# Two sums over 100,000 edges of a graph network: float32r parts, groups of four chunks, setup between steps, five parts

## The chip, the cores and the metric

The kernel runs on one core of one Trainium2 chip. The metric is the device time of one execution in microseconds (us). Three runs of the kernel before gave 4151.52, 4155.08 and 4159.06 us; the median is 4155.08.

## The reference

Four graph layers on 3125 nodes with 32 features share 100,000 edges (`src`, `dst`). Each layer takes `h = relu(layernorm(x))` and adds its result to `x`:

```
L0:  agg[src[e]] += edge_attr_32[e]                       # 32 values per edge
     x += batchnorm(relu([h, agg] @ W1.T + b1)) @ W2.T + b2
L1:  R = relu(edge_weight * w1 + b1) @ w2 + b2            # per edge, 64 -> 320
     msg = R combined with spherical harmonics of edge_attr_3 and h[src[e]]
     x[dst[e]] += msg                                     # 32 values per edge
L2:  3 rounds: out = clip(0.9 * segment_sum(norm * out[src], dst) + 0.1 * h, 0, 1)
L3:  3 rounds: z = batchnorm(relu(segment_sum(wn * z[src], dst)))
```

`norm` holds weights and weighted degrees, `wn` holds plain degrees.

## The kernel before, in words

The edges are padded to 784 chunks of 128 (an edge is a partition, a chunk is a column), and four chunks are a step: 196 steps in each of two loops. NP is 3200, the padded count of nodes.

**First sum** (`phase0` of each engine). A node number is split into a high part `a` (13 values) and a low part `b` (256 values). ScalarE makes a one-hot row of `b` for each edge in `onehots` (L510): four Squares of the distance to `iota_b`, then one Relu over the four. VectorE makes, in `products` (L921, L925), the edge's 32 values placed at its `a`: 13 x 32 = 416 columns. TensorE multiplies the two in `scatter` (L674, L678), one product for each of two parts of 128 nodes, and accumulates in PSUM. All buffers have two slots, and step s waits for the use of step s - 2.

**Matrix entries.** Beside this, the edges are written into a dense matrix `both` in HBM (two numbers for each pair of nodes: a count and a weight). GpSimd adds them by indirect DMAs with addition, one DMA per chunk (L433). Two edges of one DMA, or of DMAs in flight together, must not add to the same entry. So equal pairs of nodes inside a pair of chunks are merged first: `compare` on ScalarE (L496) makes the matrix of equal keys from a row of keys that SP loads broadcast over the partitions (L329), `mark_earlier` on VectorE (L896) finds the first of each, `merge` on TensorE (L658) sums the weights, `entries` and `entry_places` on VectorE (L905, L916) write values and places. One pair of chunks is merged per step, in both loops together 392. `add_pair` on GpSimd (L427) waits for its places and until the pair before has been added. GpSimd starts when ScalarE's queue has zeroed `both` in 40 pieces (L473): four first, then one per step. It adds 150 pairs (FIRST), then waits for the feature table.

**Between the loops** come the dense part of L0 (L942 to L998), the layer norm, and the store of a table of node features to HBM (L340).

**Second sum** (`phase1`). GpSimd gathers the features of each edge's source, one indirect DMA per chunk (L443, four per step), and between them adds pairs: two pairs per step until it has caught up with the merging, then one. TensorE forms `R` in `radial` (L715, L721), VectorE multiplies it with the features (L1020, L1024) and reduces (L1034), and `products` and `scatter` sum the messages by `dst`, now with four parts of 128 low values and 7 high values, 7 x 34 = 238 columns.

After it, `both` is read, split and used in six rounds of dense products for L2 and L3 (L749, L799).

VectorE's setup before the first loop (L855 to L894) makes keys, `a` and `b` of both ends, the three bf16 parts of the weights, `stack_id`, the layer norm of x and the unit directions `rdir`. `s_edge` fires after all of it, and ScalarE and TensorE wait for it.

## Time and profile before

| | |
|---|---|
| profiled execution | 4156.54 us, span 4154.5 us |
| granted TensorE clock, mean | 0.936 of 2.4 GHz |
| TensorE busy (PE) | 3650.0 us, 88% |
| VectorE busy (DVE) | 2566.9 us, 62% |
| ScalarE busy (ACT) | 2213.9 us, 53% |
| GpSimd busy (POOL) | 2133.7 us, 51% |
| HBM read, written | 360.07 MB, 151.93 MB |

Times in rows are us from the start of the span unless marked ns. Matmuls are pipelined, and a busy TensorE is not one at its peak. An fp32 matmul of the code appears as two recorded matmuls. GpSimd's row of an indirect DMA is the time in which it writes the descriptors, and the transfer follows it. Idle time stands behind a row in brackets, with what ended it.

### The profile page before, as it was taken

What the parts mean: (1) busy time and instruction counts of PE and PEld (TensorE: products, weight loads), DVE (VectorE), ACT (ScalarE), POOL (GpSimd) and SP (SyncE); (2) the same over time, 40 slices, a digit from 0 to 9 for tenths busy, and PEclk for the clock granted to TensorE, in tenths of its full rate; (3) what the DMA queues carried; (4) which work ended last, traced back from release to release, by engine and by line L of the source; (5) the groups of instructions that cost most, each with busy time, mean ns of one, the idle gap of its engine ahead of it and who ended that gap; (6) DMA issues with size and microseconds to landing.
All of it is one profiled execution on the core that took longest, in us unless ns stands there. A gap on an engine that the chain in (4) does not pass through costs nothing.

```text
span 4154.5 us, 65664 instructions
## 1 busy us (share of the span) xinstructions
PE 3650.0 (88%) x15883; PEld 2396.3 (58%) x15883; DVE 2566.9 (62%) x6324; ACT 2213.9 (53%) x3662; POOL 2133.7 (51%) x1582
## 2 busy tenths in 40 slices
PE   5999999999978888889999999999999754576776
PEld 2555555555546666668888888888888411132222
DVE  6555555555547776679999999999999511101011
ACT  4776776666735555557767676767666311300000
POOL 0025555555508888888888888888888300000000
PEclk9999999999988888889999999999999988778877
DMA  8962222222212222222222222222222599978764
GB/s 296 387 237 35 34 34 34 34 35 34 35 33 39 35 34 35 35 39 49 49 49 49 49 49 49 49 49 49 49 49 49 212 426 425 412 287 343 305 252 193
DMA packets 293088, 512.62 MB, mean 123 GB/s; under 512 B 153191, under 2 KB 228584, under 8 KB 275128
## 3 DMA queue, kind: packets, MB, share of 16 engines
q1 hardware_dynamic: 132232, 323.63, 21.8%
q0 software_dynamic: 137984, 39.44, 12.1%
q10 hardware_dynamic: 22832, 149.10, 8.6%
q8 instruction: 14, 0.23, 0.0%
q14 instruction: 26, 0.21, 0.0%
HBM read 360.07 MB, written 151.93 MB: 123 GB/s over the span
## 4 chain that ended last, share of the span: by engine, by line
PE 36%; DVE 24%; issue 14%; DMA 13%; POOL 9%; DVEq 2%; ACTq 1%; ACT 1%; SPq 0%; POOLq 0%
PE ps L678 28%; DVE kept L1024 7%; PE ps L749 6%; POOL both L433 6%; DVE kept L1034 4%; DMA adj_c<-kept 4%; POOL kept L443 3%; DMA big<-adj_c 3%; DVE prod L925 3%; DMA both<-kept 2%; DVE kept L1020 2%; DMA big<-both 1%; PE ps L785 1%; DMA adj_c<-prod 1%; DMA big<-adj_w 1%
## 5 line engine op out<-in xcount | busy, mean ns | idle before, releaser
L678 PE MATMUL ps<-prod,big 128*128 128x238 f32 (+1 forms) x9408 | 2518.6, 426 | 92.7 <-DVE prod L925 80.4
L678 PEld LDWEIGHTS ps<-prod,big 128*128 128x128 f32 x9408 | 1804.6, 195 | 717.5 <-issue 517.9
L433 POOL DMA_INDIRECT both<-kept x784 | 1289.9, 1645 | 805.3 <-DMA both<-kept 297.5
L520 ACT ACTIVATE big<-big 128x1024 f32<-128x1024 f32 (+1 forms) x392 | 581.5, 1483 | 877.2 <-PE ps L678 825.2
L443 POOL DMA_INDIRECT kept<-feat_dram,kept x784 | 839.1, 1070 | 331.2 <-issue 167.8
L515 ACT ACTIVATE big<-iota_b,kept 128x256 f32<-128x256 f32 (+1 forms) x1568 | 830.4, 600 | 0.0
L721 PE MATMUL ps<-w2mix,kept 65*128 65x384 f32 x1568 | 564.1, 502 | 29.9 <-ACT kept L555 20.7
L1034 DVE TENSOR_REDUCE kept<-kept 128x80 f32<-128x1280 f32 x392 | 561.5, 1472 | 0.0
L925 DVE SCALAR_TENSOR_TENSOR prod<-iota_a,kept,attr 128x416 f32<-128x416 f32 x784 | 475.5, 647 | 46.3 <-DMA attr<-in_ea 27.8
L1024 DVE TENSOR_TENSOR kept<-ps,kept 128x384 f32<-128x384 f32 x784 | 395.6, 545 | 0.0
L721 PEld LDWEIGHTS ps<-w2mix,kept 65*128 65x128 f32 x1568 | 283.3, 191 | 193.3 <-issue 33.3
L502 ACT ACTIVATE kept<-kept 128x256 f32<-128x256 f32 x784 | 350.0, 493 | 67.5 <-DMA kept<-keys_dram 56.0
L911 DVE TENSOR_REDUCE kept<-ps 128x12 f32 (+1 forms) x392 | 64.0, 163 | 509.4 <-PE ps L669 498.0
L749 PE MATMUL ps<-big,zring 128*32 128x512 f32 (+1 forms) x1120 | 243.8, 604 | 114.6 <-DMA big<-adj_c 49.0
L925 DVE SCALAR_TENSOR_TENSOR prod<-iota_a,kept 128x238 f32<-128x238 f32 x784 | 313.1, 462 | 46.9 <-DVE kept L1043 28.5
L799 PE MATMUL ps<-big,zring 128*32 128x512 f32 (+3 forms) x400 | 187.9, 624 | 164.0 <-DMA big<-both 149.9
L1020 DVE TENSOR_TENSOR kept<-ps,kept 128x512 f32<-128x512 f32 x392 | 266.4, 680 | 0.0
L1078 DVE COPY prod<-ps 128x512 f32<-128x512 f32 x18 | 11.3, 684 | 409.7 <-PE ps L749 403.7
L507 ACT ACTIVATE kept<-kept 128x512 bf16<-128x512 f32 x392 | 247.0, 630 | 28.5
L749 PEld LDWEIGHTS ps<-big,zring 128*32 128x32 f32 x1120 | 74.1, 119 | 278.6 <-issue 250.1
L799 PEld LDWEIGHTS ps<-big,zring 128*32 128x32 f32 x400 | 45.7, 125 | 306.3 <-issue 286.9
L593 ACT ACTIVATE kept<-big 128x1600 f32<-128x1600 f32 x50 | 82.4, 1653 | 248.4 <-issue 142.9
(147 smaller groups left out, 1606.8 us busy)
## 6 DMA issues: line engine op xcount, KB each, us to landing
both<-big ACTq DMA_DIRECT2D x40, 2000.0 KB, 9.1
big<-both SPq DMA_DIRECT2D x50, 1600.0 KB, 12.6
big<-adj_c SPq DMA_DIRECT2D x48, 1600.0 KB, 9.9
big<-adj_w SPq DMA_DIRECT2D x32, 1600.0 KB, 10.1
kept<-keys_dram SPq DMA_DIRECT2D x392, 128.0 KB
adj_c<-kept ACTq DMA_DIRECT2D x42, 800.0 KB, 37.6
adj_w<-kept ACTq DMA_DIRECT2D x32, 800.0 KB, 36.7
kept<-in_wT SPq DMA_DIRECT2D x196, 128.0 KB
```

The costliest lines, as they stand in the source:

```text
L433: pool.indirect_dma_start(both, bass.IndirectOffsetOnAxis(ap=sc_idx[:, 2 * d + j:2 * d + j + 1], axis=0), sc_val[:, d, j, :], None, bounds ...
L443: pool.indirect_dma_start(gath[:, s % 2, k, :], None, feat_dram, bass.IndirectOffsetOnAxis(ap=src_i[:, 4 * s + k:4 * s + k + 1], axis=0), ...
L502: act.activation(key_gap[:, i, :], keyrow[:, q, :], ACT.Square, scale=-1.0, bias=key[:, ds(2 * d + i, 1)]).then_inc(s_gap, 1)
L515: act.activation(dist2[:, k, 0:wide], iota_b[:, 0:wide], ACT.Square, scale=-1.0, bias=bcol[:, ds(4 * s + k, 1)]).then_inc(s_dist[n], 1)
L520: act.activation(onehot[:, q, :, 0:wide], dist2[:, :, 0:wide], ACT.Relu, scale=-1.0, bias=1.0).then_inc(s_oh[n], 1)
L678: mm = pe.matmul(part_sums(n, part, width), onehot[:, q, k, part * P:(part + 1) * P], prod[:, q, k, 0:HI[n] * width], start=False, stop=Fa ...
L721: mm = pe.matmul(ps[:, 4 + k, 0:384], hidT[:, q, k * P:(k + 1) * P], w2mix[:, :], start=True, stop=True)
L749: mm = pe.matmul(ps[g:g + 32, n, 0:w], zring[:, m % 8, :], values[:, c0:c0 + w], start=(m < 4), stop=(m >= NA - 4), skip_group_check=True)
L925: V.scalar_tensor_tensor(out=prod[:, q, k, 0:HI[n] * width].rearrange("p (a m) -> p a m", a=HI[n]), in0=iota_a[:, 0:HI[n]].unsqueeze(2).br ...
L1020: V.tensor_tensor(T[:, :, 0:256].rearrange("p k (o x) -> p k o x", o=16), ps[:, 4 + 2 * g:6 + 2 * g, 0:256].rearrange("p k (o x) -> p k o ...
L1024: ins = V.tensor_tensor(T[:, k, 256:640].rearrange("p (u i x) -> p u i x", u=8, i=3), ps[:, 4 + 2 * g + k, 256:384].rearrange("p (u x) -> ...
L1034: V.tensor_reduce(res[:, q, 2 * g:2 * g + 2, 0:40], terms[:, g, :, :].rearrange("p k (o x) -> p k o x", x=16), AX, ALU.add).then_inc(s_red, 1)
```

## The change

1. `PARTS` goes from (2, 4) to (2, 5): the second sum has 5 parts of 128 low values (640) and 5 high values, 5 x 34 = 170 columns.
2. In the first sum each float32 value is split by VectorE into a high part (the lower 12 bits cleared) and the rest; both are placed (13 x 64 = 832 columns), and TensorE multiplies each with the one-hot as float32r. `prod0` and `onehot0` are float32r tensors that lie over memory the first loop doesn't use otherwise.
3. In the first loop, groups of four chunks are merged in every second step. ScalarE compares half a group per step, two chunks against 512 keys. The second loop keeps pairs. GpSimd adds four chunks without waiting between them, 88 groups before the table. The spare rows go from 2 x 128 to 4 x 128.
4. `s_edge` fires after the weight parts. Destination parts and `stack_id` follow step 0, the layer norm step 1, the squares of the directions step 2, the reciprocal and `rdir` step 3. SP loads x and the directions after two attribute loads, the weights after four. ScalarE starts the zeroing when the index and weight loads have landed, no more when the keys are in HBM. Two memsets move behind the first loop.

```diff
-PARTS = (2, 4)
+PARTS = (2, 5)
-FIRST = 150
+FIRST = 88
+            def load_group(g, slot):
+                if not first(g):
+                    sp.wait_ge(s_gap, 4 * (g - 1))
+                row = keys_dram[ds(4 * g, 4), :].rearrange("(o c) p -> o (c p)", o=1)
+                sp.dma_start(keyrow[:, slot, :], row.broadcast_to([P, 4 * P])).then_inc(s_krow[slot], 16)
-            def add_pair(d):
-                pool.wait_ge(s_idx, d + 1)
-                if d:
-                    pool.wait_ge(s_add, 32 * d)
-                for j in range(2):
-                    ...
+            def add(first_c, n):
+                pool.wait_ge(s_idx, (first_c + n) // 2)
+                if first_c:
+                    pool.wait_ge(s_add, 16 * first_c)
+                for c in range(first_c, first_c + n):
+                    pool.indirect_dma_start(both, bass.IndirectOffsetOnAxis(ap=sc_idx[:, c:c + 1], axis=0),
+                                            sc_val[:, c // 2, c % 2, :], None, bounds_check=last_entry,
+                                            compute_op=ALU.add).then_inc(s_add, 16)
-            for d in range(FIRST):
-                add_pair(d)
+            for g in range(FIRST):
+                add(4 * g, 4)
             for s in range(STEPS):
+                if s + 1 < STEPS:
+                    gather(s + 1, (0, 1))
+                n = 4 if added < CH // 2 else 2
+                if added + n <= 2 * (STEPS + s + 1 - BEHIND):
+                    add(added, n)
+                    added += n
+                if s + 1 < STEPS:
+                    gather(s + 1, (2, 3))
+                if CH // 2 <= added <= 2 * (STEPS + s - BEHIND):
+                    add(added, 2)
+                    added += 2
+            def compare_group(g, s, slot, half):
+                ...
+                for i in (2 * half, 2 * half + 1):
+                    act.activation(key_gap[:, i % 2, :], keyrow[:, slot, :], ACT.Square, scale=-1.0,
+                                   bias=key[:, ds(4 * g + i, 1)]).then_inc(s_gap, 1)
+                act.wait_ge(s_gap, 2 * s + 2)
+                if half == 0 and not first(g):
+                    act.wait_ge(s_ded, 2 * g - 2)
+                act.activation(same[:, slot, 2 * half:2 * half + 2, :], key_gap[:, :, :], ACT.Relu, scale=-1.0,
+                               bias=1.0).then_inc(s_same, 1)
+            def merge_group(g, slot):
+                ...
+                for j in range(4):
+                    pe.matmul(o[:, j, 0:1], same_tri[:, slot, j, :], ones_bf[:, :], ...)
+                    for i in range(4):
+                        mm = pe.matmul(o[:, j, lo:7], same[:, slot, i, j * P:(j + 1) * P], ...)
             def scatter(n, s, q, k, width):
                 ...
+                    else:
+                        for t in range(2):
+                            mm = pe.matmul(part_sums(n, part, width), onehot0[:, q, k, mine],
+                                           prod0[:, 4 * q + k, :, t, :], start=False, stop=False,
+                                           skip_group_check=True)
+            def split_products(s, q, k):
+                if not first(s):
+                    dve.wait_ge(s_sum[0], 4 * s - 8 + k + 1)
+                V.scalar_tensor_tensor(
+                    out=prod0[:, 4 * q + k, :, :, :].rearrange("p a t m -> p a (t m)"),
+                    in0=iota_a[:, 0:HI[0]].unsqueeze(2).broadcast_to([P, HI[0], 2 * FEAT]),
+                    scalar=a_src[:, ds(4 * s + k, 1)],
+                    in1=rows0[:, q, k, :, :].rearrange("p t m -> p (t m)").unsqueeze(1)
+                    .broadcast_to([P, HI[0], 2 * FEAT]),
+                    op0=ALU.is_equal, op1=ALU.mult).then_inc(s_prod[0], 1)
+            def phase0(s, k4, u):
+                q, g, slot = k4 % 2, u * 2 + k4 // 2, k4 // 2
+                if q:
+                    mark_group(g, slot)
+                dve.wait_ge(s_attr[q], 32 * u + 16 * slot + 16)
+                V.tensor_scalar(rows0[:, q, :, 0, :].bitcast(I32), attr[:, q, :, :].bitcast(I32), -4096, None,
+                                ALU.bitwise_and).then_inc(s_hi, 1)
+                dve.wait_ge(s_hi, s + 1)
+                V.tensor_tensor(rows0[:, q, :, 1, :], attr[:, q, :, :], rows0[:, q, :, 0, :],
+                                ALU.subtract).then_inc(s_rows, 1)
+                dve.wait_ge(s_rows, s + 1)
+                for k in range(4):
+                    split_products(s, q, k)
+                    if q and k == 2:
+                        group_entries(g, slot)
+                if q:
+                    group_places(g)
```

`mark_group`, `group_entries` and `group_places` are `mark_earlier`, `entries` and `entry_places` over four chunks.

## Rows read from the trace of the kernel before

**Rows 1.** Timeline, one step of the first sum: start us, us, engine, line.

```profile
601.69 5.83 PE L678 MATMUL ps<-prod,big 128*128 128x416 f32 x16
602.99 0.28 DVE L902 TENSOR_TENSOR kept<-kept,earlier 128x256 bf16<-128x256 bf16 x1
603.19 1.77 DVE L925 SCALAR_TENSOR_TENSOR prod<-iota_a,kept,attr 128x416 f32<-128x416 f32 x3
603.77 0.63 ACT L507 ACTIVATE kept<-kept 128x512 bf16<-128x512 f32 x1
604.31 1.69 ACT L515 ACTIVATE big<-iota_b,kept 128x256 f32<-128x256 f32 x4
607.51 5.83 PE L678 MATMUL ps<-prod,big 128*128 128x416 f32 x16
```

**Rows 2.** Windows: stretch, length, busy PE, PEld, DVE, ACT, POOL, PEclk, DMA share, GB/s.

```profile
60.00:260.00 200.00, 200.00 (x761) 109.49 (x759) 103.50 (x277) 141.72 (x272) 0.00 (x0) 1.00 0.96 381
1213.00:1224.00 11.00, 10.37 (x49) 10.37 (x49) 1.45 (x8) 0.00 (x0) 0.00 (x0) 0.50 0.01 1
2000.00:3000.00 1000.00, 1000.00 (x4880) 812.65 (x4880) 967.03 (x2441) 698.86 (x1062) 806.00 (x637) 1.00 0.29 49
```

**Rows 3.** Timeline of GpSimd where the second sum turns to single pairs.

```profile
1824.19 1.09 POOL L443 DMA_INDIRECT kept<-feat_dram,kept  x1 [0.31 <-issue]
...
1829.61 1.62 POOL L433 DMA_INDIRECT both<-kept  x1 [0.30 <-issue]
...
1833.42 1.10 POOL L443 DMA_INDIRECT kept<-feat_dram,kept  x1 [0.31 <-issue]
```

**Rows 4.** Timeline of GpSimd: first and last add ahead of the table, first gather.

```profile
268.84 1.69 POOL L433 DMA_INDIRECT both<-kept  x1 [263.27 <-DMA both<-big]
...
1146.55 1.66 POOL L433 DMA_INDIRECT both<-kept  x1 [0.30 <-issue]
1240.38 1.10 POOL L443 DMA_INDIRECT kept<-feat_dram,kept  x1 [92.17 <-DMA feat_dram<-big]
```

**Rows 5.** Timeline: the dense part's first operation, the last gather.

```profile
1195.88 0.99 DVE L945 COPY big<-h 128x800 f32<-128x800 f32 x1 [4.90 <-PE ps L678]
...
3249.24 1.05 POOL L443 DMA_INDIRECT kept<-feat_dram,kept  x1 [0.30 <-issue]
```

**Rows 6.** Timeline of TensorE: bf16 opening, small fp32 products, second sum.

```profile
1208.84 0.61 PE L654 MATMUL ps<-zero_bf 128*128 128x512 bf16 x2
1213.63 10.88 PE L711 MATMUL ps<-w2T,big 128*128 128x32 f32 x50 [4.18 <-DVE big L967]
...
2206.58 6.69 PE L678 MATMUL ps<-prod,big 128*128 128x238 f32 x32
```

**Rows 7.** Groups by line and shape, whole span: count, busy us, mean ns.

```profile
L515 ACT ACTIVATE big<-iota_b,kept 128x512 f32<-128x512 f32 x784 | 499.3, 707 | 0.0
L925 DVE SCALAR_TENSOR_TENSOR prod<-iota_a,kept,attr 128x416 f32<-128x416 f32 x784 | 475.5, 647 | 46.3 <-DMA attr<-in_ea 27.8 <-PE ps L678 3.1
L515 ACT ACTIVATE big<-iota_b,kept 128x256 f32<-128x256 f32 x784 | 331.0, 493 | 0.0
L925 DVE SCALAR_TENSOR_TENSOR prod<-iota_a,kept 128x238 f32<-128x238 f32 x784 | 313.1, 462 | 46.9 <-DVE kept L1043 28.5 <-issue 18.2
```

**Rows 8.** Timeline of the setup: the last weight part, the last directions.

```profile
21.88 1.68 DVE L877 CAST kept<-big 128x784 bf16<-128x784 f32 x1
...
44.26 2.61 DVE L892 TENSOR_TENSOR kept<-big 128x2352 f32<-128x2352 f32 x1
```

**Rows 9.** DMA issues from 60 to 260 us: count, KB each, median us to landing.

```profile
both<-big ACTq DMA_DIRECT2D x34, 2000.0 KB, 9.0
```

**Rows 10.** Timeline of GpSimd and VectorE around two adds of the first loop.

```profile
560.12 1.54 POOL L433 DMA_INDIRECT both<-kept  x1 [0.30 <-issue]
...
562.60 1.78 DVE L925 SCALAR_TENSOR_TENSOR prod<-iota_a,kept,attr 128x416 f32<-128x416 f32 x3
...
563.94 1.84 POOL L433 DMA_INDIRECT both<-kept  x1 [2.28 <-DMA both<-kept]
```

More of the change, by code:

```diff
@@ L19 @@
 F32 = mybir.dt.float32
+F32R = mybir.dt.float32r
 BF16 = mybir.dt.bfloat16
@@ L179, in gnn_program, with placed_at @@
         big = sb("big", [P, 4, NP])
+        big_end = nc.sbuf_base
+        def placed_at(name, shape, end):
+            n = 4
+            for d in shape[1:]:
+                n *= d
+            return nc.alloc_sbuf_tensor_at(name, shape, F32R, offset=end - n)
+        prod0 = placed_at("prod0", [P, 8, HI[0], 2, FEAT], kept_end)
+        onehot0 = placed_at("onehot0", [P, 2, 4, PARTS[0] * P], big_end - 4 * (2 * NP - 2 * 4 * PARTS[0] * P))
         zeros = big[:, 0, :]
@@ L336, in load0 @@
                              ea32_in[:, ds(s * (4 * FEAT), 4 * FEAT)]).then_inc(s_attr[q], 16)
-            steps(sp, load0)
+            for s in range(2):
+                load0(s, s, 0)
+            sp.dma_start(x[:, :, :], x_in.rearrange("(a b) f -> b a f", b=P)).then_inc(s_in["x"], 16)
+            sp.dma_start(rel[:, :, :], ea3_in).then_inc(s_in["rel"], 16)
+            for s in range(2, 4):
+                load0(s, s, 0)
+            for dst, src in loads:
+                sp.dma_start(dst, src).then_inc(s_in["wts"], 16)
+            with sp.Fori(1, STEPS // 4) as u:
+                for k4 in range(4):
+                    load0(u * 4 + k4, k4, u)
             sp.wait_ge(s_table, 1)
@@ L560, in phase1 @@
                 onehots(1, s, q, b_dst)
+            act.wait_ge(s_edge, 2)
             steps(act, phase1)
@@ L660, in merge @@
                 pe.wait_ge(s_tri, d + 1)
-                if not first(d):
-                    pe.wait_ge(s_idx, d - 1)
+                pe.wait_ge(s_idx, d - 1)
                 o = ps[:, 2 + q, 0:14].rearrange("p (j v) -> p j v", j=2)
@@ L894, in _, with mark_group @@
-            dve.wait_ge(s_edge, 1)
+            V.tensor_copy(wparts[:, :, 6], wrest).then_inc(s_edge, 1)
+            dve.wait_ge(s_edge, 1)
+            def mark_group(g, slot):
+                dve.wait_ge(s_same, 2 * g + 2)
+                if not first(g):
+                    dve.wait_ge(s_ded, 2 * g - 2)
+                within = same[:, slot, :, :].rearrange("p i (j e) -> p (i j) e", j=4)[:, 0:16:5, :]
+                V.tensor_tensor(same_tri[:, slot, :, :], within,
+                                earlier[:, :].unsqueeze(1).broadcast_to([P, 4, P]), ALU.mult).then_inc(s_tri, 2)
@@ new lines, in group_entries @@
+            def group_entries(g, slot):
+                dve.wait_ge(s_ded, 2 * g + 2)
+                if not first(g, 1):
+                    dve.wait_ge(s_idx, 2 * g)
+                m = ps[:, 2 + slot, 0:28].rearrange("p (j v) -> p j v", j=4)
+                V.tensor_reduce(sc_val[:, ds(2 * g, 2), :, :].rearrange("p d j v -> p (d j) v"),
+                                m[:, :, 1:7].rearrange("p j (v i) -> p j v i", i=3), AX, ALU.add)
+                V.scalar_tensor_tensor(out=offs[:, :], in0=m[:, :, 0], scalar=0.0, in1=to_spare[:, ds(4 * g, 4)],
+                                       op0=ALU.is_gt, op1=ALU.mult).then_inc(s_offs, 2)
@@ new lines, in _ @@
+            dve.wait_ge(s_keysd, 16)
+            phase0(0, 0, 0)
+            link(V.tensor_scalar(tmp_i, dst_i[:, :], 7, None, ALU.arith_shift_right))
+            link(V.tensor_scalar(b_dst.bitcast(I32), tmp_i, 205, None, ALU.mult))
+            link(V.tensor_scalar(tmp_i, b_dst.bitcast(I32), 10, None, ALU.arith_shift_right))
+            link(V.tensor_copy(a_dst[:, :], tmp_i))
+            V.scalar_tensor_tensor(out=b_dst[:, :], in0=a_dst[:, :], scalar=-640.0, in1=dst_i[:, :],
+                                   op0=ALU.mult, op1=ALU.add).then_inc(s_edge, 1)
@@ new lines, in _ @@
+            link(V.tensor_tensor(stack_id[:, :], ident[:, 0:32], ident[:, 32:64], ALU.add))
+            link(V.tensor_tensor(stack_id[:, :], stack_id[:, :], ident[:, 64:96], ALU.add))
+            link(V.tensor_tensor(stack_id[:, :], stack_id[:, :], ident[:, 96:128], ALU.add))
+            phase0(1, 1, 0)
+            dve.wait_ge(s_in["x"], 16)
+            layernorm()
+            phase0(2, 2, 0)
+            dve.wait_ge(s_in["rel"], 16)
+            link(V.tensor_tensor(rinv[:, :], rel[:, :, 0], rel[:, :, 0], ALU.mult))
@@ L943, in _ @@
+            link(V.tensor_tensor(rdir[:, :, 2:5], rel[:, :, :],
+                                 rinv[:, :].unsqueeze(2).broadcast_to([P, CH, 3]), ALU.mult))
+            with dve.Fori(1, STEPS // 4) as u:
+                for k4 in range(4):
+                    phase0(u * 4 + k4, k4, u)
             dve.wait_ge(s_in["wts"], 16 * 12)
             dve.wait_ge(s_sum[0], CH)
+            V.memset(res[:, :, :, 41:42], 1.0)
+            link(V.memset(hidT[HID1:HID1 + 1, :, :], 1.0))
             V.tensor_copy(cat[:, :, 0:32], h[:, :, :])
```

217 lines of the change are left out of this document (109 added, 108 removed).

## The prediction

> **What bounds the kernel now.** I read the busy tenths of the page first, then the windows, the waits of each engine, the timelines of single steps, and last GpSimd's queue from end to end. The page's totals name TensorE (3650.0 of 4154.5 us), and the chain's largest line is its product L678 (28%); both mislead, for the loops have different limits.
>
> *First sum (196 steps, L686).* The next step's 16 passes begin 5.82 us after this one's [rows 1], and TensorE is busy in all 200 us of 60 to 260 [rows 2]. One fp32 product of 416 columns is two recorded passes, 5.83/16 = 0.35 us each, two clocks a column. VectorE and ScalarE have slack, GpSimd adds pairs beside them.
>
> *Second sum (196 steps, L729).* Here VectorE is busy 967 and GpSimd 806 of 1000 us [rows 2], and GpSimd's indirect DMAs follow each other with a gap of only 0.30 us, so its queue is full although the share says 81%. Its own pace for a step of four gathers and two adds is 1833.42 - 1824.19 = 9.23 us; the two adds take 1833.42 - 1829.61 = 3.81 of it, so an add costs 1.905 and a gather (9.23 - 3.81)/4 = 1.355 us [rows 3]. 106 steps in the 1000 us make 9.43 a step. Before that, 43 steps carry four adds each (L457 lets GpSimd catch up), and VectorE idles for gathers.
>
> So one queue runs through both loops. GpSimd waits for zeroed memory until 268.84, does 150 pairs until 1148.2, waits for the feature table until 1240.38 [rows 4], and its last gather ends at 3250.3 [rows 5]. Between: 784 gathers (1062 us) and 478 adds (911) are 1973 us of 2010; 37 are holds and waits. What comes later (904 us) the change leaves alone.
>
> **The first sum's step after.** *TensorE* has 16 float32r passes of 416 columns. No row shows this type. Lower bound: two bf16 products of 512 columns take 0.61 us in all [rows 6], near one clock a column, which would be 416/2.4 = 0.17 us here; upper bound: a pass as now, 0.35. I take 0.18, nearer to bf16, because float32r is given only numbers already cut to a short part, and a single product of it is to do what two passes did. That is 2.9 us, with ten small products a step (six cost 5.82 - 16 x 0.35 = 0.2 now) 3.2; at the upper bound 6.0. The Trainium skill ("FP8 and Floating Point Precision", TensorE Precision Notes) says that true fp32 takes four passes and reduced precision truncates to 22 bits; that counts two clocks a column in each of the two rows recorded, and by it the step is 3.2.
>
> *VectorE.* Products start 0.566 us apart at 416 elements ((1.77 - 0.65)/2 [rows 1]), and an element costs 1.04 ns ((647 - 462)/178 [rows 7]). Of 832 elements: 1.00 us, four 4.0. Two linked operations of 128 elements form the parts: nearest row 0.28 each [rows 1], with the link 0.6 (bounds 0.3 and 0.8). Marking and entries, once in two steps but on four chunks, about 0.42 a step. Sum 5.03 us.
>
> *ScalarE.* Compare now squares 512 columns: they start 0.614 apart (256 columns: (1.69 - 0.49)/3 = 0.40 [rows 1]; a column (707 - 493)/256 = 0.84 ns [rows 7]), so both with 0.07 of link make 1.39; the Relu over 1024 columns then keeps the engine 0.96 (512 columns: 0.54 [rows 1]); four squares of 256 take 1.72, their Relu 0.96. Sum 5.03 too. With two slots per buffer neither blocks the other much; I take 5.08 a step, bounds 4.9 (an engine runs ahead) and 5.5 (they wait in turn).
>
> *Setup.* `s_edge` fires after the weight parts: VectorE ends them at 23.56 now, less four casts of 0.6, at 21.2; it was at 46.9 [rows 8]. But stack_id, layer norm, squares, reciprocal and directions move between steps 0 to 3, still on VectorE, which is the bound now: 46.9 - 23.6 plus the destination columns, 25.5 us. Its cover is gone, so nothing is gained but the early start of TensorE. Step 4 begins near 21.2 + 25.5 + 4 x 5.03 = 67, say 70 with first loads. On SP the loads of x and of directions now follow two attribute loads, the weights' follow four; they land long before their users.
>
> *Zeroing* puts one piece of 2 MB per step into steps 4 to 39; until 260 the DMA engines are busy 96% [rows 2] at 5.83 us a step, 5.6 us of work. Faster steps don't make these transfers faster: 5.7 a step, last piece issued near 70 + 35 x 5.7 = 270, zeroed at about 276 (bounds 257 and 285; a piece lands in 9.0 us [rows 9]).
>
> End of the sum: 70 + 36 x 5.7 + 156 x 5.08 = 1068. The dense part from 1195.88 to the first gather is 44.5 us; the moved memsets add 1 on VectorE. Table ready: 1113.
>
> **The adds (FIRST = 88 groups).** GpSimd waits for the adds in flight once per four instead of once per two. One add is 1.54 and 0.30 [rows 10], the wait 2.2 to 2.3: 3 x 1.84 + 1.54 + 2.2 = 9.26 us. A pair should be 5.6 so, but 150 took 879.4, 5.86 each. Rows 10 show why: the add at 560.12, with no product of VectorE under its start, took 1.54; that at 563.94 began inside the third product from 562.60 and took 1.84, that is, it was held until the product ended at 564.38. Holds are 0.13 us per add now. After, products are 1.08 instead of 0.65 us long and fill 80% of VectorE's time instead of 40%; a random start finds 0.3 to 0.4 left, the following adds start a little before a product's end, 0.15 to 0.25. I take 0.21 per add, a group at 10.1 us; bounds 9.45 (0.05 each) and 10.9 (0.4 each). 88 groups: 889 us, less 8 for the stretch after VectorE's products have ended. 276 + 881 = 1157, later than the table (1113): the adds bind. The Trainium skill ("SBUF — State Buffer", SBUF: two separate sides) has a port pair that VectorE with two SBUF inputs and a GpSimd operation reading SBUF take for a whole instruction; the trace agrees (0.30 us more), and it speaks against this change, since one longer product holds longer. Without it the group would be 9.26 and the table would bind.
>
> **The second sum.** TensorE: five products of 170 columns a chunk, two passes each, instead of four of 238. A pass of 238 is at most 6.69/32 = 0.21 us [rows 6], 0.203 by columns (238/1.2 ns + 5); of 170, 0.147. Each pass loads 128 columns of weights: with hardly any columns to stream that took 10.88/50 = 0.218 us [rows 6] at a granted clock of 0.50 (1.2 GHz) [rows 2], so by an estimate 0.109 at full clock, below 0.147. 40 x 0.147 against 32 x 0.203: 0.6 us less, about 8.7 a step. Were it 0.218 here, a step would be 11.5 us and the time 1157 + 2254 + 904 + 2 = 4317; the full clock of [rows 2] in this loop, where TensorE stays 94% busy, speaks against it. VectorE: 4 x 68 x 1.04 ns = 0.28 less, 9.15. ScalarE: 4 x 128 + 512 columns more, 0.85 us, with 301 of 1000 us free. All are below GpSimd's 9.23, so GpSimd sets this loop; the gain per single step is 9.43 - 9.3, not TensorE's 0.6. Its work is what counts: 352 adds done before, so 426 up to the last gather instead of 478, and 16 steps with more than two adds instead of 43. 1062 + 426 x 1.905 = 1874, holds 19 (37 now), 1893 us (bounds 1874 and 1920).
>
> **Sum.** Last gather 1157 + 1893 = 3050 against 3250.3; the last step is half a microsecond shorter. The profiled execution's 4156.5 (span 4154.5 and 2.0 around it; median 4155.1) becomes **3956**.
>
> **Rivals.** *Holds fade.* For: the second to fourth add of a group may all start as one product ends. Against: the hold in [rows 10], on a shorter product. Group 9.45, adds end at 1108, the table binds at 1113: last gather 3006, 3912 us. *TensorE stays the bound in the first sum*: float32r passes at 0.35, or the clock falls to 1.2 GHz because TensorE works 3.2 of 5.1 us, which gives 416/1.2 = 0.35 as well. For: the granted clock is full only where it is always busy; against: its pauses would be below 1 us. 6.0 us a step: about 70 + 192 x 6.0 = 1222, table 1267, last gather 3160, 4066 us. *GpSimd is starved* (the other side): each add waits out a whole 1.0 us product. Group 9.26 + 4.0 = 13.3, first gather 1443, last 3336, 4242 us. It turns slower when a group costs over (1357 - 276)/88 = 12.3 us, a hold of 0.76 per add; the rows show 0.3 at most of a 0.65 product, which is against it.
>
> **How the numbers follow.** Forecast 0.60, holds fade 0.16, TensorE bound 0.16, starved or bound by weight loads 0.04, the rest (the same mechanisms, other sizes) 0.04. The forecast alone spans 3910 (zeroed at 257, group 9.9) to 4010 (285, 10.6). Range 3885 to 4070, which takes in the first two rivals. About 0.2% can be told from no change; faster 0.94, same 0.01, slower 0.05.
>
> **What would show it.** Steps of the first sum 5.0 to 5.2 us apart after 280, VectorE and ScalarE above 95% there and TensorE's recorded products near 0.18 apart; first add at 270 to 285; groups of four 10.1 us apart with adds of 1.6 to 1.9; last add of the first loop near 1157 and the first gather right behind it with no wait for the table; 16 steps of 13 us, then steps of 9.25 to 9.35 with VectorE waiting for gathers. It is wrong if the first gather waits for the table, if float32r passes are 0.35, or if single steps keep 9.43.

## The result, and the profile after

The changed kernel took **3977.2 us** (median of four runs, 3961.4 to 3986.6) against 4155.6 us of the kernel before: a ratio of 0.9567 with a 95% interval of [0.9535, 0.9599]. The profiled execution took 3975.5 us (span 3973.8); the forecast was 3956, so it is 19.5 us late, and the median 21.2.

First the page of the changed kernel: engine totals and three of its costliest groups.

```profile
PE 3210.8 (81%) x18235; PEld 2332.3 (59%) x18235; DVE 2874.9 (72%) x6330; ACT 2549.9 (64%) x3663; POOL 2152.9 (54%) x1582
...
L461 POOL DMA_INDIRECT both<-kept x784 | 1300.4, 1659 | 701.6 <-DMA both<-big 263.5
...
L470 POOL DMA_INDIRECT kept<-feat_dram,kept x784 | 847.6, 1081 | 239.2 <-issue 180.1
...
L1016 DVE SCALAR_TENSOR_TENSOR prod<-iota_a,kept,prod 128x832 fp32r<-128x832 f32 x784 | 805.9, 1080 | 48.7 <-DVE prod L1032 47.8
```

TensorE has lost 439 us of its 3650, the profiled time only 181. The windows (columns as in [rows 2], which holds the ones of before) tell where the limits lie:

```profile
60.00:260.00 200.00, 149.90 (x896) 118.16 (x894) 174.21 (x278) 173.56 (x279) 0.00 (x0) 0.91 0.96 386
600.00:1000.00 400.00, 342.34 (x2061) 238.43 (x2059) 377.35 (x630) 389.63 (x632) 267.34 (x154) 1.00 0.32 39
2000.00:3000.00 1000.00, 951.66 (x5777) 797.73 (x5776) 952.35 (x2461) 798.27 (x1070) 804.34 (x642) 0.99 0.32 49
```

In the first sum ScalarE is busy 389.6 and VectorE 377.4 of 400 us (with the 20 us that it waits for its own parts, L1032, it is full too), TensorE 342.3: its bound has passed to the two others, at 5.08 us a step (by the starts of VectorE's products). In the second sum 642 GpSimd instructions stand in 1000 us, six a step: 9.35 us a step, against 9.43.

GpSimd's queue from end to end, to be laid beside [rows 4, 5] (timeline: start, us, and in brackets what it waited for):

```profile
269.18 2.49 POOL L461 DMA_INDIRECT both<-kept  x1 [263.49 <-DMA both<-big]
...
1178.91 1.54 POOL L461 DMA_INDIRECT both<-kept  x1 [0.30 <-issue]
1180.76 1.09 POOL L470 DMA_INDIRECT kept<-feat_dram,kept  x1 [0.31 <-issue]
```

The first gather follows the last add with no wait for the table, as forecast, and the last gather starts at 3072.7. Four stretches make up the account:

| stretch | forecast | measured |
|---|---|---|
| zeroed, first add | 276 | 269.2 |
| 352 adds up to the first gather | 881 | 911.6 |
| first to the end of the last gather | 1893 | 1893.0 |
| from there to the end of the span | 904 less 0.5 | 900.0 |

So the miss is one term: the adds, 30.6 us too dear, less 6.8 for the earlier zeroing and nearly 4 at the end.

### The profile page after: what moved, and what is told of

Read it like the earlier page. It is cut to its first block, busy times and chain, and to the rows that moved or that the text cites. A ratio compares the mean times of both kernels' runs of the same rounds, so it can differ in the third digit from the quotient of the medians.

```text
span 3973.8 us, 69047 instructions
## 1 busy us (share of the span) xinstructions
PE 3210.8 (81%) x18235; PEld 2332.3 (59%) x18235; DVE 2874.9 (72%) x6330; ACT 2549.9 (64%) x3663; POOL 2152.9 (54%) x1582
## 4 chain that ended last, share of the span: by engine, by line
POOL 38%; DMA 35%; issue 13%; PE 9%; DVE 3%; ACT 1%; ACTq 0%; another core or an unknown queue 0%; SPq 0%; DVEq 0%; POOLq 0%
POOL both L461 22%; DMA both<-kept 21%; POOL kept L470 16%; PE ps L827 7%; DMA adj_c<-kept 4%; DMA big<-adj_c 2%; DMA big<-both 2%; DVE prod L1016 1%; PE ps L863 1%; DMA attr<-in_ea 1%; DMA big<-adj_w 1%; DMA adj_c<-prod 1%; PE ps L750 1%; DMA kept<-keys_dram 1%; DMA adj_w<-kept 1%
## 5 line engine op out<-in xcount | busy, mean ns | idle before, releaser
L745 PE MATMUL ps<-prod,big 128*128 128x170 f32 x7840 | 1221.8, 317 | 119.9 <-DVE prod L1006 119.8
L745 PEld LDWEIGHTS ps<-prod,big 128*128 128x128 f32 x7840 | 1172.4, 195 | 238.9 <-DVE prod L1006 229.1
L750 PE MATMUL ps<-prod,onehot 128*128 128x416 f32 x3136 | 776.9, 385 | 222.7 <-ACT onehot L564 123.3
L559 ACT ACTIVATE big<-iota_b,kept 128x256 f32<-128x256 f32 (+1 forms) x1568 | 914.8, 654 | 0.0
L1016 DVE SCALAR_TENSOR_TENSOR prod<-iota_a,kept,prod 128x832 fp32r<-128x832 f32 x784 | 805.9, 1080 | 48.7 <-DVE prod L1032 47.8
L750 PEld LDWEIGHTS ps<-prod,onehot 128*128 128x128 f32 x3136 | 553.2, 194 | 420.0 <-DVE prod L1016 369.7
L564 ACT ACTIVATE big<-big 128x2560 f32<-128x2560 f32 x196 | 458.0, 2337 | 376.2 <-PE ps L745 376.2
L799 PE MATMUL ps<-w2mix,kept 65*128 65x384 f32 x1568 | 564.0, 503 | 24.3 <-ACT kept L604 20.5
L1006 DVE SCALAR_TENSOR_TENSOR prod<-iota_a,kept 128x170 f32<-128x170 f32 x784 | 258.1, 392 | 56.2 <-DVE kept L1177 56.1
L546 ACT ACTIVATE kept<-kept 128x512 f32<-128x512 f32 x392 | 259.2, 708 | 20.7 <-DMA kept<-keys_dram 20.1
## 6 DMA issues: line engine op xcount, KB each, us to landing
big<-both SPq DMA_DIRECT2D x50, 1600.0 KB, 12.3
big<-adj_w SPq DMA_DIRECT2D x32, 1600.0 KB, 10.1
```

The source lines that it names most:

```text
L559: act.activation(dist2[:, k, 0:wide], iota_b[:, 0:wide], ACT.Square, scale=-1.0, bias=bcol[:, ds(4 * s + k, 1)]).then_inc(s_dist[n], 1)
L564: act.activation((onehot0, onehot)[n][:, q, :, 0:wide], dist2[:, :, 0:wide], ACT.Relu, scale=-1.0, bias=1.0).then_inc(s_oh[n], 1)
L745: mm = pe.matmul(part_sums(n, part, width), onehot[:, q, k, mine], prod[:, q, k, 0:HI[n] * width], start=False, stop=False, skip_group_che ...
L750: mm = pe.matmul(part_sums(n, part, width), onehot0[:, q, k, mine], prod0[:, 4 * q + k, :, t, :], start=False, stop=False, skip_group_chec ...
L799: mm = pe.matmul(ps[:, 4 + k, 0:384], hidT[:, q, k * P:(k + 1) * P], w2mix[:, :], start=True, stop=True)
L1016: V.scalar_tensor_tensor(out=prod0[:, 4 * q + k, :, :, :].rearrange("p a t m -> p a (t m)"), in0=iota_a[:, 0:HI[0]].unsqueeze(2).broadcast ...
```

## Why a group of adds takes two steps

This is the timeline of one group, VectorE and GpSimd together, in order of time:

```profile
514.39 1.08 DVE L1016 SCALAR_TENSOR_TENSOR prod<-iota_a,kept,prod 128x832 fp32r<-128x832 f32 x1
514.72 2.19 POOL L461 DMA_INDIRECT both<-kept  x1 [2.26 <-DMA both<-kept]
516.27 4.07 DVE L1016 SCALAR_TENSOR_TENSOR prod<-iota_a,kept,prod 128x832 fp32r<-128x832 f32 x4 [0.26 <-DVE prod L1032]
517.21 1.56 POOL L461 DMA_INDIRECT both<-kept  x1 [0.30 <-issue]
519.08 1.69 POOL L461 DMA_INDIRECT both<-kept  x1 [0.30 <-issue]
521.07 1.54 POOL L461 DMA_INDIRECT both<-kept  x1 [0.30 <-issue]
...
524.55 1.07 DVE L1016 SCALAR_TENSOR_TENSOR prod<-iota_a,kept,prod 128x832 fp32r<-128x832 f32 x1
524.82 2.24 POOL L461 DMA_INDIRECT both<-kept  x1 [2.21 <-DMA both<-kept]
```

The first add starts 0.33 us into a product, and takes 2.19 instead of 1.54 us: held until the product ends. The next group starts in the same product two steps later (524.55 - 514.39 = 10.16) and is held again (2.24). If it came a little earlier, it would be held longer; if later, less. So the group does not draw its holds at random: it would take 9.26 us of its own, comes earlier into the loop's steps until its holds (0.65 us at the first add and 0.15 at the third here) make up what is missing to two steps, and stays there. I call this a **lock**. The median group of the loop is 10.2 us, two steps are 10.16, and of the groups within the first sum 80% begin within 0.3 us of two steps after the one before. The same stood in the profile of before: steps start 5.82 us apart in [rows 1], and I had put a pair at 5.86 from [rows 4]; its median is 5.83. I had read that as 5.60 plus 0.26 of random holds.

That the forecast of 10.1 per group came out near was therefore luck. The experiments were made to see what holds the group, and what each part of the change is worth.

## The experiments

Times are medians; ratios are to the kernel before, in runs beside it, with 95% intervals. Figures of groups are of the first loop, all four adds and their wait, the twelve or so behind the first sum included. The runs of the changed kernel alone span 25 us, and the intervals of e1, e2, e3, e8, e9 and e10 overlap with its own: what these kernels tell is read from their groups and stretches, not from their times.

| kernel | us | ratio | step, first sum | group, mean | first gather |
|---|---|---|---|---|---|
| changed | 3977.2 | 0.957 [0.954, 0.960] | 5.08 | 10.39 | 1180.8 |
| e1 rows in PSUM | 3965.7 | 0.953 [0.948, 0.958] | 5.13 | 10.15 | 1168.4 |
| e2 83 groups | 3953.7 | 0.950 [0.945, 0.956] | 5.08 | 10.36 | 1126.7 |
| e3 slower ScalarE | 3990.3 | 0.959 [0.954, 0.964] | 5.27 | 10.51 | 1192.2 |
| e4 fp32 product | 4024.3 | 0.967 [0.961, 0.972] | 5.87 | 9.83 | 1244.6 |
| e5 key halves | 4051.1 | 0.975 [0.971, 0.980] | 5.54 | 10.87 | 1256.0 |
| e6 PSUM, key halves | 4013.7 | 0.965 [0.961, 0.970] | 5.54 | 9.70 | 1218.8 |
| e7 wait per pair | 4194.0 | 1.009 [1.006, 1.012] | 5.08 | 12.78 | 1391.7 |
| e8 four parts | 3987.5 | 0.958 [0.954, 0.962] | 5.08 | 10.29 | 1180.6 |
| e9 PSUM, early halves | 3968.5 | 0.953 [0.949, 0.957] | 5.13 | 10.19 | 1171.7 |
| e10 setup first | 3966.4 | 0.953 [0.949, 0.957] | 5.08 | 10.32 | 1190.9 |
| e11 fp32, 98 groups | 4100.9 | 0.985 [0.979, 0.990] | 5.87 | 9.81 | 1246.2 |
| e12 step of 6 us | 4179.1 | 1.004 [1.001, 1.007] | 6.01 | 10.39 | 1270.5 |

**e1: row parts in PSUM.**

```diff
-rows0 = prod_all[:, 21 * P:21 * P + 8 * 2 * FEAT].rearrange(...)
+rows0 = ps[:, 4, :].rearrange("p (q k t f) -> p q k t f", q=2, k=4, t=2)
```

> The two parts of each row that the first sum's products read (the high and the low half of 128x128) lie in PSUM instead of SBUF, so VectorE's product of 832 elements has one input in SBUF. Theory (an add of GpSimd that starts inside a VectorE operation with two SBUF inputs is held until that operation ends): adds back at 1.54 to 1.6 us, groups of four at 9.3 instead of 10.15, the 88 groups through by about 1110, so that the feature table (1112) or the last add binds, first gather at 1112 to 1125, time 3905 to 3925. Rival A (any VectorE work holds an add, whatever it reads): groups stay at 10.15, time 3977. Rival B (a PSUM input makes the product longer, over 1.1 us): steps of the first sum longer than 5.07 us, the table later than 1130, time 3935 or more.

The holds went, the group's length did not. A stretch of its GpSimd timeline, and of the loads that SP issued beside it:

```profile
637.53 1.54 POOL L461 DMA_INDIRECT both<-kept  x1 [0.31 <-issue]
639.38 1.54 POOL L461 DMA_INDIRECT both<-kept  x1 [0.30 <-issue]
644.17 1.54 POOL L461 DMA_INDIRECT both<-kept  x1 [3.25 <-DMA both<-kept]
```

```profile
639.13 0.33 SPq L353 DMA_DIRECT2D attr<-in_ea  x1
640.01 0.33 SPq L345 DMA_DIRECT2D kept<-keys_dram  x1
```

Adds average 1.56 us instead of 1.74, with products as long as before (1.076 us): it is the second SBUF input that holds them, and rival A falls. The Trainium skill ("SBUF — State Buffer", SBUF: two separate sides) says that a VectorE operation with two SBUF inputs and a GpSimd operation that reads SBUF lock each other out of a shared port pair; the trace agrees: 178 adds of e1 start inside a product, and their mean is 0.001 us over 1.54, against 0.28 in the changed kernel. But the wait for the last add grew from 2.43 to 2.95 us in the mean. Here it stands behind 64 KB of attributes and 256 KB of key rows, issued 0.25 us before and 0.63 us after the last add's start; within the first sum a group takes 10.22 us in the mean, and two groups in a row 20.5, which is four steps of 5.13: the lock is still there. A lock needs only something periodic that delays: with the products gone as an obstacle, the loads may have become it. That the loads delay the completion is read from such rows, not tried alone: it would take a loop without them. The 88 groups took 20.8 us less than in the changed kernel (890.8 against 911.6), but the first add came 8.4 us later (277.6), so the first gather came only 12.4 us earlier, and the time of 3965.7 is far from the theory's 3905 to 3925.

**e5, e6, e9: the key rows in two halves of 128 KB.** e5 alone, e6 with the rows in PSUM; e9 as e6, with the first half issued a step earlier.

```diff
-sp.dma_start(keyrow[:, slot, :], row.broadcast_to([P, 4 * P]))
+sp.dma_start(keyrow[:, slot, 2 * P * half:2 * P * (half + 1)],
+             row.broadcast_to([P, 2 * P]))     # half 0 and 1 in two steps
```

> The key rows of a group, one broadcast load of 256 KB in two steps, are loaded as two halves of 128 KB in two steps following each other; nothing else. In e1_psum_rows the adds took 1.54 us, but the wait for their completion was 2.95 us in the mean (2.2 where nothing else moves), behind such a load. Theory (with products that read SBUF the holds alone stretch the group to two steps): groups stay at 10.15, first gather 1170 to 1182, time 3965 to 3979. Rival (the load of 256 KB is what stretches a group here too): groups at 9.9 or less, first gather before 1160, time below 3957.

> Both together: the row parts in PSUM and the key rows in halves. Theory (GpSimd's group slips against the two steps of the loop until something holds it, either a product with two SBUF inputs or a long load behind its last add; with both gone it runs at its own pace): waits of 2.2 to 2.6 us, groups at 9.3 to 9.6, the 88 groups done by 1095 to 1120, then the table (first sum 5.11 us a step there, table at about 1127) sets the first gather, time 3920 to 3935. Rival (something else still ties it to two steps, or each half load holds it as much): groups at 10.0 or more, time 3955 to 3970.

> As e6_psum_key_halves (row parts in PSUM, key rows in halves), but the first half of a group's key rows is issued one step earlier, so that ScalarE no longer waits for the second half (it did, 32 us in 400, and made the step 5.55 us and the first gather wait 65 us for the table). Theory: first sum at 5.1 to 5.15 us a step, table at 1122 to 1132, groups at 9.3 to 9.8 and 88 of them done by 1130, first gather 1125 to 1135, last gather 3018 to 3028, time 3918 to 3932. Rival (the key loads hold the adds as soon as they don't wait for ScalarE): groups at 10.1, tied to two steps, first gather 1165 or later, time 3955 to 3970.

My edit made the second half arrive late in e5 and e6, so that ScalarE waited, the first sum's step grew to 5.54 us and the first add came only at 302 to 303 us. The waits of e6 between 600 and 1000 us show it:

```profile
engine line waited for: us in total, times, longest us
...
ACT kept L552 <- DMA kept<-keys_dram: 32.1, 18, 2.4
```

This spoiled the times and what e5 was to tell, but it moved the period of the loop, which tells something else. In e5, with products still holding, groups run in twos: from 429.5 to 451.5 it takes 22.0 us for two, and four steps are 22.2; neither outcome that I had put down. In e6, with no product to hold, the median is 9.37, near the group's own 9.26, for the first time (mean 9.70, just above the 9.3 to 9.6 of its theory). All its 88 groups were done at 1153.5, later than the 1120 that I had put down because they began 33 us later, and the table came only at 1218.8. And e9, where the halves arrive in time and the step is 5.13 again, is back at 10.23 us in the mean within the first sum and 20.5 for two groups: the rival of e9, with its first gather at 1171.7 and its 3968.5 us. So the loads in halves hold a group (its wait is 3.0 us in the mean) as well as one load does. That e6 was freed by its longer period is the likeliest reading, but its halves were also issued at another place in the step, and no run parts the two.

**e3, e12: the loop slowed on ScalarE**, by one copy of 128 columns and by two of 448.

```diff
+act.activation(idle[:, :], iota_b[:, 0:EXTRA], ACT.Copy)
 onehots(0, s, k4 % 2, b_src)
```

> One more copy of 128 columns on ScalarE in each step of the first sum (0.29 us; its result is not used), which holds no add and only makes the step 5.36 us. Theory (in the loop the groups of adds are locked to two steps: holds stretch the 9.26 us until the period is that of two steps): groups of four at 10.7 us, first gather at 1215 to 1230, time 4012 to 4028. Rival (holds are met at random, 0.21 per add as I put it in the prediction): groups at 10.0 to 10.15, the products fill less of VectorE's time, first gather 1175 to 1181, time 3971 to 3980, for the first sum's end (1111) and the table (1156) stay ahead of the last add.

> The changed kernel with two more copies of 448 columns on ScalarE in each step of the first sum (results not used), so that its step is about 5.95 us and two steps 11.9, with VectorE's products of 832 elements as they are. Theory (a group of adds locks to two steps only as long as the holds in its way can fill the difference to 9.26 us: 0.9 at 10.14, 1.3 at 10.53, but not 2.6; at 11.1 in e5_key_halves groups already alternated between 9.7 and 12.5): groups spread over 9.3 to 12.5, mean 10 to 10.6, last add near 1190 to 1210, then a wait for the table (ready near 1262), time 4050 to 4070. Rival (they lock all the same): median within 0.1 of two steps (11.9), last add near 1310 behind the table, first gather there, time 4100 to 4120.

The copy cost 0.19 us a step, not 0.29. Two steps are 10.55, and the median group became 10.54 (10.19 in the changed kernel): a loop slowed on an engine that holds no add stretched the typical group by nearly as much. Random holds would have left it at 10.15 or less. The mean within the first sum grew less, from 10.40 to 10.60, since the changed kernel has longer outliers; so the first gather (1192.2) and the time (3990.3) lie between what theory and rival had put down. Here two such groups of e3, whose adds are held in other places each time:

```profile
717.80 1.54 POOL L463 DMA_INDIRECT both<-kept  x1 [2.95 <-DMA both<-kept]
719.64 1.96 POOL L463 DMA_INDIRECT both<-kept  x1 [0.30 <-issue]
...
728.64 1.67 POOL L463 DMA_INDIRECT both<-kept  x1 [3.19 <-DMA both<-kept]
...
738.76 1.54 POOL L463 DMA_INDIRECT both<-kept  x1 [2.82 <-DMA both<-kept]
```

They last 10.84 and 10.12 us, 10.48 in the mean: the lock is looser than in the changed kernel, and the loads take part. At 6.01 us a step (e12) the missing 2.75 us are more than it was held for; groups spread from 9.45 to 12.3, mean 10.39, and the last add ends at 1196.9, as expected. The time did not: see e11.

**e7: a wait after each pair again.**

```diff
-for g in range(FIRST):
-    add(4 * g, 4)
+for g in range(2 * FIRST):
+    add(2 * g, 2)
```

> In the first loop GpSimd waits for its adds after each pair again instead of after each four; all else as in the changed kernel. Theory (one wait of 2.2 us less in four adds is what the merging gives to GpSimd): a pair 5.58 us plus holds of 0.2 per add, 5.9 to 6.0, so 11.8 to 12.0 for four adds, first gather 1305 to 1325, time 4100 to 4120. Rival (the pace is tied to the loop anyway, so the wait costs nothing): 10.15 for four, 3977.

It costs 217 us, not 123 to 143. A pair needs 5.6 us of its own, more than a step, so it locks to a longer pattern: its timeline repeats after three pairs.

```profile
307.77 1.67 POOL L461 DMA_INDIRECT both<-kept  x1 [2.45 <-DMA both<-kept]
...
328.06 1.67 POOL L461 DMA_INDIRECT both<-kept  x1 [2.45 <-DMA both<-kept]
...
348.32 1.72 POOL L461 DMA_INDIRECT both<-kept  x1 [2.41 <-DMA both<-kept]
...
388.96 1.68 POOL L461 DMA_INDIRECT both<-kept  x1 [2.45 <-DMA both<-kept]
```

The rows are 20.29, 20.26 and (six pairs) 40.64 us apart, and four steps are 20.30: 6.77 for a pair, 13.5 for four adds. With a wait after each pair and all the rest, 88 groups ahead of the table included, the kernel is slower than before (by 0.6 to 1.2%). The saving of TensorE made the loop's period one that fits pairs badly. That is not the best that pairs could do, though: the table is ready near 1112, and 98 adds fewer ahead of it would have brought the first gather from 1391.7 to about 1127. At 1.6 (e2) to 1.9 us (the prediction's price) for each in the second sum, that is an estimated 4086 to 4116 us, above the changed kernel and below the one before. No run tried it.

**e2: 83 groups instead of 88.**

```diff
-FIRST = 88
+FIRST = 83
```

> FIRST is 83 groups instead of 88, so 20 adds move from the stretch where GpSimd waits for its own adds to the second sum, where gathers lie between. Theory (GpSimd's queue sets the time): the first gather at 1125 to 1135 instead of 1180.8 (5 groups of 10.0 us less), still behind the table, the last gather at 3062 to 3066 instead of 3073.8, since 20 adds cost 38 us there; time 3965 to 3969. Rival (in the second sum VectorE or TensorE takes over while GpSimd catches up, so adds there are free or gathers are late anyway): time 3977 within 3, or a gain of over 20 us, 3955.

```profile
1124.85 1.54 POOL L461 DMA_INDIRECT both<-kept  x1 [0.30 <-issue]
1126.70 1.09 POOL L470 DMA_INDIRECT kept<-feat_dram,kept  x1 [0.30 <-issue]
...
3050.67 1.05 POOL L470 DMA_INDIRECT kept<-feat_dram,kept  x1 [0.31 <-DMA both<-kept]
```

The first gather comes 54 us earlier and the second sum lasts 32 us longer for 20 more adds, 1.6 us each; the last gather starts 22.0 us earlier, more than the 8 to 12 expected: 4 more because five groups cost 54 and not 50, the rest in the second sum, where the adds were put at 38. The order of events is as theory had it, but the time fell out of its 3965 to 3969 and onto the rival's 3955, whose reason was that adds in the second sum cost less than their own work. Here they cost 1.6 us where theory had 1.9, not nothing; that difference is no larger than the spread of the second sum between kernels (see e8), so one kernel does not decide it. At 3953.7 us it is the fastest kernel of the study, 0.6% below the changed one; the two intervals overlap by a little.

**e4, e11: one fp32 product again,** first with 88 groups, then with 98.

```diff
-prod0 = placed_at("prod0", [P, 8, HI[0], 2, FEAT], kept_end)    # float32r, high part and rest
+prod0 = placed_at("prod0", [P, 8, HI[0], FEAT], kept_end)       # float32, no parts
-for t in range(2): pe.matmul(..., prod0[:, 4 * q + k, :, t, :], ...)
+pe.matmul(..., prod0[:, 4 * q + k, :, :], ...)
```

> Only the split is undone: the first sum has one fp32 product of 416 elements per chunk and one fp32 matmul, no parts, the groups of four, the five parts and the moved setup stay. Theory: TensorE is the bound of the first sum again at 5.9 us a step, VectorE's products are 0.65 us and hold less, groups at 9.6 to 9.9 us, 88 groups done by 1135, but the sum ends near 1200 and the table is ready near 1247, first gather there, last gather near 3140, time 4035 to 4050. Rival (the first sum's own speed does not count since GpSimd sets both loops, only the number of adds done before): first gather 1135, time 3930. Second rival (float32r brought nothing to TensorE's pace, merging in fours did): step below 5.3 us, time below 3990.

> As e4_fp32_product (one fp32 product and one fp32 matmul per chunk, no split), with FIRST at 98 groups instead of 88. In e4_fp32_product GpSimd had its 88 groups done at 1135.3 us and waited 109 us for the table. Theory (what GpSimd has done before the table is ready is what counts): ten more groups at 9.8 us fit into that wait and end near 1234, the first gather stays at 1240 to 1248, the second sum has 40 adds less at 1.85 us each (74 us), time 3945 to 3958, as fast as the float32r kernel with 83 groups (3953.7) and faster than the changed kernel. Rival (float32r itself is what makes the kernel fast, the adds at the end are hidden behind the gathers): time 4010 to 4025.

```profile
1133.75 1.54 POOL L461 DMA_INDIRECT both<-kept  x1 [0.30 <-issue]
1244.63 1.09 POOL L470 DMA_INDIRECT kept<-feat_dram,kept  x1 [109.34 <-DMA feat_dram<-big]
```

In e4 the adds are faster than in the changed kernel (groups 9.83: shorter products, and a period of 11.7 us too far from 9.26), but GpSimd then stands still for 109 us. So float32r brings nothing to the queue itself; it brings the table forward by 133 us, and of those only what GpSimd can use counts: 47 us. (The time is 11 us below the expected 4035, mostly by a second sum of 1879.4 us between the gathers' starts instead of 1893.) In e11 the first loop went as expected: 98 groups done at 1233.0, first gather at 1246.2. But the second sum lasted 1951.1 us, where 1805 was expected, and the kernel took 4100.9. Its steps are 10.0 us (599 instructions of GpSimd in 1000 us), and e12 has the same 599. About every fourth step looks like this (e11: windows, then rows of its timeline):

```profile
2065.00:2070.00 5.00, 5.00 (x41) 4.95 (x41) 4.91 (x12) 3.95 (x7) 3.96 (x4) 1.00 0.41 63
2070.00:2075.00 5.00, 2.70 (x9) 1.28 (x8) 1.89 (x2) 1.86 (x1) 4.09 (x4) 0.86 0.19 30
2075.00:2080.00 5.00, 2.98 (x10) 2.98 (x11) 4.25 (x18) 4.58 (x9) 3.87 (x3) 0.50 0.27 57
```

```profile
2073.14 2.34 ACT L564 ACTIVATE big<-big 128x2560 f32<-128x2560 f32 x1 [4.20 <-remote]
...
2077.02 7.67 PE L745 MATMUL ps<-prod,big 128*128 128x170 f32 x40 [4.33 <-DVE prod L1005]
...
2082.34 1.02 POOL L470 DMA_INDIRECT kept<-feat_dram,kept  x1 [2.86 <-DVE kept L1150]
```

ScalarE pauses 4.2 us ahead of its Relu, TensorE is idle for 4.33 us, the granted clock falls to 0.50 (1.2 GHz), and its 40 passes take 7.67 us instead of 5.9. What stops ScalarE the profile does not name, and no run tells it; e4 and e6 waited long for the table too and kept 9.3 us a step. From 1300 to 3050 us e11 has 43 such pauses of over 2 us, e12 48, e7 11, and the other changed kernels at most 4. The 146 us that e11's second sum is too long are 3.4 for each of its pauses. e11 and e12 also ran on one chip and no other kernel of the change did, though the kernel before took its usual 4154.6 us there; whether the chip has a part in it was not tried. **This stays open.** Until it is known, e11 shows only that the adds fit into the wait, not that the time follows.

**e8: four parts in the second sum.** It leaves out the nodes whose low part lies in the fifth of the five.

```diff
-PARTS = (2, 5)
+PARTS = (2, 4)
```

> The second sum has four parts of 238 columns again instead of five of 170; all else as in the changed kernel. Theory (GpSimd's queue sets the pace, but TensorE and VectorE at 967 of 1000 us hold its gathers now and then): single steps at 9.43 us instead of 9.35, about 168 of them, 10 to 18 us more, time 3987 to 3996. Rival A (GpSimd alone counts there): 3977 within 4. Rival B (TensorE binds with four parts): steps at 9.6 or more, time 4020 or more.

```profile
2000.00:3000.00 1000.00, 999.90 (x4879) 812.60 (x4880) 967.21 (x2440) 698.87 (x1061) 805.72 (x637) 1.00 0.28 49
```

The first gather is where it was (1180.6), the second sum is 18.6 us longer (1910.5 between the first and the last gather's starts, against 1891.9), steps 9.42 against 9.35, and TensorE is busy all the time. In the eight other kernels with the same 426 adds and steps of 9.2 to 9.4 us (e1, e3 to e7, e9, e10) that stretch lasts 1874 to 1898 us, so by this one profile four parts cost 13 to 37. The time of 3987.5 is as theory had it.

**e10: the setup in one piece ahead of step 0.**

```diff
+link(...)                     # destination columns, stack_id, layernorm(), squares, rdir
+for s in range(4):
+    phase0(s, s, 0)
-phase0(0, 0, 0) ... phase0(1, 1, 0) ... phase0(2, 2, 0) ... phase0(3, 3, 0)
```

> The moved setup (destination columns, stack_id, layer norm, squares, reciprocal, directions) stands ahead of step 0 on VectorE and its two roots ahead of step 0 on ScalarE, as before the change; all else as in the changed kernel. Theory (VectorE sets the first steps, so moving its setup between them gains only what TensorE starts earlier, which is idle there anyway): step 0's first product near 47 us instead of 21.3, step 4 within 3 us of 70.5, zeroing and first add within 3 us of 269, time 3974 to 3982. Rival (the zeroing follows the early steps, or the transfers of the setup were a cover): first add 15 to 25 us later, time 3992 to 4002.

Step 0's first product came at 59.8 us (47 expected), step 4's at 84.5 instead of 71.3. The first add moved by 16.8 us, into the rival's range, and the first gather by 10.1:

```profile
285.96 1.81 POOL L461 DMA_INDIRECT both<-kept  x1 [280.27 <-DMA both<-big]
```

In step 4 ScalarE waits 10.5 us for its key row, and its queue, which issues the zeroing, with it. Of the 16.8 us only the 13 up to step 4 are sure, for with step 4 at 71.1 to 71.7 the first add came at 269.2 to 270.1 in the changed kernel, e2, e3 and e7, and at 278.1 in e8, whose first loop is the same. The time is not longer for it (3966.4, below both forecasts), because this execution's second sum is one of the short ones (1873.9): a spread of 20 us that the runs show without naming its cause is larger than what the moved setup is worth.

## Why the prediction was right, and where it was not

- **One queue through both loops** held. The first gather follows the last add, the last gather ends at 3073.8, and what comes later took 900.0 us (904.2 before). e2 is the clean test: five groups fewer, the first gather 54 us earlier, the last gather 22 us.
- **The first sum's step** (5.08) was 5.08; VectorE's products are 1.00 us apart as worked out. Step 4 began at 70.5 (70). Four float32r passes start 0.16 to 0.17 apart (their weight loads of 0.19 us span 0.68), so the bound fell as forecast, and the rival that kept TensorE as the bound is out: the granted clock was 1.00 from 600 to 1000 us although TensorE is idle for a seventh of them. That was nearer than it looks: with steps of 5.27, 5.54 and 6.01 us (e3, e5, e12) the granted clock of the same stretch was 0.88, 0.89 and 0.87. (The prediction's 5.83/16 is 0.364, not 0.35; the 0.35 is two clocks a column, as the rest of its sum uses it.)
- **The group of four** (10.1) failed as a mechanism. The step "holds are 0.21 per add, at random" has in its place a lock to the loop: two steps of 5.08, 10.16 us (in e3 to its own longer two, in e7 of three pairs to four). As a size the typical group was right, by luck. The prediction's lower end of the forecast alone, zeroed at 257 and a group of 9.9, adds up to 3919 and not 3910, which changes nothing in its range. The other 20 us of the 76 groups within the first sum, which average 10.4, are a few long ones, of which the longest begins so:

```profile
555.35 2.16 POOL L461 DMA_INDIRECT both<-kept  x1 [2.29 <-DMA both<-kept]
560.61 2.22 POOL L461 DMA_INDIRECT both<-kept  x1 [3.10 <-issue]
...
571.59 1.54 POOL L461 DMA_INDIRECT both<-kept  x1 [3.93 <-DMA both<-kept]
```

  A gap of 3.1 us with nothing that GpSimd waits for by the profile. Counted in adds it stands ahead of number 113 (from 0), and in this and all twelve other changed kernels a gap of 1.7 to 3.6 us stands ahead of adds 113, 226 and 339 (as far as their first loop goes), whatever the time (560.6 here, 612.3 in e5), and a wait of 2.8 to 4.9 us ahead of 60, 120, 180, 240 and 300. So they belong to places in GpSimd's own instructions, not to the loop beside it; what happens there (a load of instructions would fit) the profile does not say. Each also throws the group out of its lock, and the next one or two are long.
- **"Less 8 behind the first sum"** was wrong by 7: twelve groups of 10.0 instead of 9.3 to 9.4, mostly by the store of the table (one wait of 6.56 us, at 1108.2) and the pauses just named.
- **The setup "gains nothing"** was wrong in its reason: VectorE's work is the same, but the zeroing and the key rows start earlier, worth 13 us at step 4, up to 17 on the first add and 10 on the first gather (e10). The forecast had the benefit anyway, since it took step 4 at 70.
- **The second sum** (1893.0) was met to the microsecond, which is partly chance, for the same work took 1874 to 1898 in other kernels. That the fifth part gains "9.43 - 9.3, not TensorE's 0.6" is right in kind (e8: 9.42 against 9.35).
- **GpSimd starved** did not come, but e7 shows its like: one wait more and the lock falls on a pattern of 13.5 us for four adds (12.78 in the mean), above the turning point of 12.3 that the prediction gave, and the kernel is indeed slower than before.

## What to carry to other kernels

When a queue with a fixed cycle of its own runs beside a loop that can delay it, compare its period with the loop's: if a small multiple of the loop's is a little longer than its own (0.9 us here, while at 2.75 in e12 it ran free), it can be locked, and its price is then the loop's period, not its own work plus average delays. Then taking away one delay brings little (e1: 21 us of 912), because the next obstacle takes over. And where work can stand before or after a point that waits for another engine, move just as much ahead of it as fits into the wait (e2).

## What the hardware did that I had not expected

- An add of GpSimd is held by what VectorE runs when the add starts, and in 217 of 234 such adds of the changed kernel until that operation ends; back-to-back products do not hold it on. But 15 of the 17 that started in a product followed by the marking operation (bf16, two SBUF inputs) were held through that one too (0.62 us with 0.27 left of the product). Beside 1.08 us products an add lost up to 0.95 us (adds of 1.54 to 2.49), and nothing once the product read one input from PSUM.
- An add that starts in the first 0.03 us of a product is not held: 22 such adds of e3 all took 1.54 us.
- That PSUM input made the products no longer (1.076 against 1.080 us).
- Completion of an add took 2.1 to 2.3 us on a quiet DMA system, and up to 6.6 when a store of 1.2 MB was under way.
- In e11 the granted clock went from 1.00 to 0.50 behind a pause of TensorE of 4.33 us, and the 40 passes that followed took 7.67 us instead of 5.9. With about every fourth step paused like this, steps are 10.0 us in the mean, not 9.35.
